# The wavelet stage in another order: TensorE's step in three runs, restoring and token work a step later, twelve input buffers

## The chip, the core and the metric

The kernel runs on one core of one Trainium2 chip. Five engines of the core run their own instruction queues, each strictly in the order in which the program wrote them: TensorE (PE; its weight loads are shown apart as PEld), VectorE (DVE), ScalarE (ACT), GpSimd (POOL) and the sync engine (SP), which here only issues DMAs. They meet at semaphores. The metric is the device time of one execution in microseconds, and the lower the better; the time of a kernel is the median of its runs.

## What is computed

The input `x` is a float32 tensor of 4 images, 64 channels, 128 by 128 points. Four blocks run one after the other, each with a residual sum:

```python
x = x + _L0_conv_ref(_ln_c(x), ...)      # Haar wavelet, 64x256 and 256x64 products, inverse wavelet
t = t + _L0_ffn_ref(_ln_t(t), ...)       # 32 experts, each picks the 8 best tokens of an image
x = x + _L1_conv_ref(_ln_c(x), ...)      # four directional scans with a 9-tap convolution
t = t + _L1_ffn_ref(_ln_t(t), ...)       # 8 experts, each token picks 2
```

The change touches only the program's first large stage. That stage takes `_ln_c` (mean and variance over the 64 channels of a point), the wavelet block as two matrix products ("low" and "restore") with the residual sum, which gives `x1`; and then, of `x1` as tokens, the layer norm `_ln_t`, the gate's logits and the running best eight of each expert. The later stages (expert choice, four scans, mixture) are as before.

## The kernel before

`wavelet_mixer` cuts the input into 64 chunks (`CHUNKS`) of 128 partitions by 512 columns (64 channels of an even and of an odd image row). Each engine has a loop over steps `c`; in a step it works on several chunks of different age. On TensorE a step of before holds, in this order:

- `centre(c)`, lines 412 and 413: `x` minus its mean over the channels, as two fp32r products, of the rounded part `xh` and of the rest `xl`, into the bank `xc`;
- `variance(c-1)`, lines 418 and 419: the same for the square of `xc`, parts `sqh` and `sql`, into `va`;
- `low(c-2)`, line 427: two f32 products that each use 64 columns of the array, into the bank `tv`;
- in even steps only, `gate_logits` (line 434, bank `lg`) and `token_variance` (line 441, bank `tv` again), for a pair of chunks, also 64 columns wide;
- `turn(c-3)`, line 455: four transposes of the finished `x1` into `tt`;
- `token_centre(c-4)`, lines 448 and 449: `x1` minus its mean, two fp32r products, parts `th` and `tl`, into `tc`;
- `restore(c-2)`, line 462: two f32 products of 256 columns into `rec`.

A step with the logits is called *heavy* below and one without them *light*; they alternate.

The other engines' parts of a step, in their order. ScalarE: `square(c)` (490), the logarithm of the variance (495), `copy_low(c-2)` (506, it empties the first half of `tv`), the exponential (499), `high_of_token(c-3)` (511, makes `th`), in even steps `token_rstd` (516 and 518), and `token_square(c-4)` (523). VectorE: `add_restored(c-3)` (581, makes `x1`), `high_of_square(c)` (588, makes `sqh`), `high_of_x(c+2)` (575), `scale_logits` (605) or `block_top` (611) in turn, `normalise(c-1)` (593), `copy_tokens(c-3)` (598). GpSimd has three subtractions: `low_of_square(c)` (545, makes `sql`), `low_of_x(c+2)` (550, makes `xl`), `low_of_token(c-3)` (556, makes `tl`). SP loads the chunk three steps ahead (367) and stores `x1` in two layouts (381 and 385).

So there is a ring through four engines: `centre` on TensorE, `square` on ScalarE, `high_of_square` on VectorE, then GpSimd, whose in-order queue has `low_of_square`, `low_of_x` and `low_of_token` behind one another, and back to TensorE. The wait with which `token_centre` takes the end of that queue is

```python
def token_centre(c):
    wait(pe, s["tparts"], c + 1)
    wait(pe, s["tsquared"], c)
```

and `token_variance(pair, c)`, which writes the bank that `low(c)` has just filled, waits for ScalarE's copy of it: `wait(pe, s["low_s"], min(c + 1, CHUNKS))`.

`metaformer_kernel` lays out the buffers and calls the stages; ten input buffers `xr` and ten semaphores `xin` go round.

Of the kernel before, what the change touches and what calls it, by code (L numbers as in the profile page):

```python
# [37 lines left out]
SLOT = B * HP * WP  # L38
TOK = HP * W
E0, HID, K0 = 32, 256, 8  # L40
XBUFS = 10
AHEAD = 3
E1 = 8
TAPS = 9
# [281 lines left out]

def wavelet_mixer(nc, g, a):

    LAG = 5
    PAIRS = CHUNKS // 2  # L330
    with ExitStack() as ctx:
        m = Mem(nc, ctx, "wm")
# [25 lines left out]
        with nc.Block() as block:  # L358
            @block.sync
            def _(sp):  # L360
                def load(c):
                    wait(sp, x1_out[c % XBUFS], c // XBUFS * 16)
                    wait(sp, s["tturned"], c - XBUFS + 1)
                    wait(sp, s["logits"], (c - XBUFS) // 2 * 2 + 2)
                    wait(sp, s["tparts"], c - XBUFS + 1)
                    for t in range(2):
                        sp.dma_start(buf(c)[t * C:t * C + C].rearrange("p (j w) -> p j w", j=JR),
                                     x_chunk(a, c, t)).then_inc(xin[c % XBUFS], 16)

                def load_experts(q):  # L370

                    e = slice(q * E0 // 8, (q + 1) * E0 // 8)
                    sp.dma_start(g.W1[0:C + 1, e], a["weight1"][e].rearrange("e d h -> d e h")
                                 ).then_inc(g.experts_loaded, 16)
                    for t in range(2):
                        sp.dma_start(g.W2[:, e, t, :], a["weight2"][e, t * P:t * P + P, :].rearrange(
                            "e p o -> p e o")).then_inc(g.experts_loaded, 16)

                def store_x1(c):
                    wait(sp, s["x1"], c + 1)  # L380
                    sp.dma_start(g.x1s[c:c + 1].rearrange("t p n -> p (t n)"), buf(c)).then_inc(x1_out[c % XBUFS], 16)

                def store_tokens(c):
                    wait(sp, s["tcopied"], c + 1)
                    sp.dma_start(tok_dst[c % B][:, c // B * JR:c // B * JR + JR, :],
                                 ts[c % 4].rearrange("p (j x) -> p j x", j=JR)).then_inc(tok_out[c % 4], 16)

                for sem in g.setup_sems:
                    sp.sem_clear(sem)
                for c in steps:  # L390
                    if now(c + AHEAD):
                        load(c + AHEAD)
                    if 8 <= c < 16:
                        load_experts(c - 8)
                    if now(c - 3):
                        store_x1(c - 3)
                    if now(c - 4):
                        store_tokens(c - 4)
                for u in range(XBUFS):
                    sp.wait_ge(x1_out[u], 16 * len(range(u, CHUNKS, XBUFS)))  # L400
                for u in range(4):
                    sp.wait_ge(tok_out[u], 16 * (CHUNKS // 4))
                sp.wait_ge(g.late_loaded, 16 * 6)

            @block.tensor
            def _(pe):
# [14 lines left out]
                def low(c):  # L421
                    wait(pe, s["normed"], c + 1)
                    wait(pe, s["low_s"], c)
                    wait(pe, s["tln"], (c - 3) // 2)
                    nv = nn[c % 2].rearrange("p (q v) -> p v q", v=2)
                    for v in range(2):
                        last = pe.matmul(tv[v * C:v * C + C, 0:N // 2], g.Alow[:, v], nv[:, v], start=True, stop=True)
                    last.then_inc(s["low"], 1)
# [8 lines left out]
                def token_variance(pair, c):  # L437
                    wait(pe, s["tsquared"], 2 * pair + 2)
                    wait(pe, s["low_s"], min(c + 1, CHUNKS))
                    for half in range(2):  # L440
                        last = pe.matmul(tv[half * C:half * C + C, :], g.J[:, C - E0:C + E0], tsq[half],
                                         start=True, stop=True)
                    last.then_inc(s["tvar"], 2)

# [21 lines left out]
                for c in steps:  # L466
                    if now(c):
                        centre(c)
                    if now(c - 1):
                        variance(c - 1)  # L470
                    if now(c - 2):
                        low(c - 2)
                    if now(c - 5) and c % 2 == 0:
                        gate_logits((c - 5) // 2)
                        token_variance((c - 5) // 2, c - 2)
                    if now(c - 3):
                        turn(c - 3)
                    if now(c - 4):
                        token_centre(c - 4)
                    if now(c - 2):  # L480
                        restore(c - 2)

            @block.scalar
            def _(act):
# [34 lines left out]

                def token_square(c):  # L520
                    wait(act, s["tcentred"], c + 1)
                    wait(act, s["tvar"], c - 1)
                    act.activation(tsq[c % 2], tc[:], ACT.Square).then_inc(s["tsquared"], 1)

                for c in steps:
                    if now(c):
                        square(c)
                    if now(c - 1):
                        log_of_variance(c - 1)
                    if now(c - 2):  # L530
                        copy_low(c - 2)
                    if now(c - 1):
                        rstd(c - 1)
                    if now(c - 3):
                        high_of_token(c - 3)
                    if now(c - 5) and c % 2 == 0:
                        token_rstd((c - 5) // 2)
                    if now(c - 4):
                        token_square(c - 4)

            @block.gpsimd
            def _(pool):
                def low_of_square(c):
                    wait(pool, s["high"], c + 1)
                    pool.tensor_tensor(sq_lo[:], sq[c % 2], sq_hi[:].bitcast(F32), ALU.subtract).then_inc(s["parts"], 1)  # L545

                def low_of_x(c):
                    wait(pool, s["xhigh"], c + 1)
                    wait(pool, s["centred"], c - 1)
                    pool.tensor_tensor(xl[c % 2][:], buf(c), xh[c % 2][:].bitcast(F32), ALU.subtract  # L550
                                       ).then_inc(s["xparts"], 1)

                def low_of_token(c):
                    wait(pool, s["thigh"], c + 1)
                    wait(pool, s["tcentred"], c - 1)
                    pool.tensor_tensor(tl[c % 2], buf(c), th[c % 2].bitcast(F32), ALU.subtract
                                       ).then_inc(s["tparts"], 1)
                for c in range(2):
                    low_of_x(c)
                for c in steps:  # L560
                    if now(c):
                        low_of_square(c)
                    if now(c + 2):
                        low_of_x(c + 2)
                    if now(c - 3):
                        low_of_token(c - 3)

            @block.vector
            def _(dve):
                dve.tensor_copy(Cmr[:], g.Cm[:]).then_inc(exact_ready, 1)  # L570

                def high_of_x(c):
                    wait(dve, xin[c % XBUFS], c // XBUFS * 32 + 32)
                    wait(dve, s["centred"], c - 1)
                    dve.tensor_copy(xh[c % 2][:], buf(c)).then_inc(s["xhigh"], 1)

# [36 lines left out]
                for c in range(2):  # L613
                    high_of_x(c)
                for c in range(CHUNKS + LAG + 2):
                    if now(c - 3):
                        add_restored(c - 3)
                    if now(c):
                        high_of_square(c)
                    if now(c + 2):  # L620
                        high_of_x(c + 2)
                    if now(c - 6) and c % 2 == 1:
                        scale_logits((c - 6) // 2)
                    if c >= 8 and c % 2 == 0:
                        block_top((c - 8) // 2)
                    if now(c - 1):
                        normalise(c - 1)
                    if now(c - 3):
                        copy_tokens(c - 3)

# [1151 lines left out]
def metaformer_kernel(nc, a, out):  # L1784
    g = Shared()
    with ExitStack() as ctx:
# [8 lines left out]
        g.experts_loaded, g.late_loaded = m.sem("experts_loaded"), m.sem("late_loaded")  # L1795

        g.mix_loaded = m.sem("mix_loaded")
        g.xin = m.sems("xin", XBUFS)
        g.taps_loaded, g.unit_ready, g.taps_turned, g.taps_hi, g.taps_cleared = (
            m.sem(f"w_{n}") for n in ("ld", "id", "tn", "hi", "clr"))  # L1800
        g.blank = {1: m.sem("w_b1"), 2: m.sem("w_b2")}
# [3 lines left out]

        v = Views(g.X, 0)
        g.xr = [v.take(N) for _ in range(XBUFS)]
        g.sq, g.rr, g.nn, g.tsq = ([v.take(N) for _ in range(2)] for _ in range(4))
        g.lowS = [v.take(N // 2) for _ in range(2)]
        g.ts = [v.take(N) for _ in range(4)]  # L1810
        g.trs = v.take(N)
# [60 lines left out]
```

## Time and profile before

| | us |
|---|---|
| time, median of 3 runs | 2098.15 (2095.51 to 2099.45) |
| the profiled execution | 2100.63 |
| its span in the trace | 2098.8 |
| TensorE busy | 1984.3 (95% of the span) |
| VectorE, ScalarE, GpSimd busy | 1201.0, 1035.5, 592.4 |
| wavelet stage, first chunk's second subtraction to the next stage's first instruction | about 18 to 316 |

The span runs from the first to the last instruction of the profile. An engine's busy time counts the length of its instructions; matmuls are pipelined, so that a TensorE that is busy all the time need not be at its peak, and where matmuls follow one another the distance of their starts says what one costs. In the wavelet stage TensorE is shown as busy without a gap, and the three other engines for 84 to 87% of the time.

### The profile page before, as it was taken

What the parts mean: (1) busy time and instruction counts of PE and PEld (TensorE: products, weight loads), DVE (VectorE), ACT (ScalarE), POOL (GpSimd) and SP (SyncE); (2) the same over time, 40 slices, a digit from 0 to 9 for tenths busy, and PEclk for the clock granted to TensorE, in tenths of its full rate; (3) what the DMA queues carried; (4) which work ended last, traced back from release to release, by engine and by line L of the source; (5) the groups of instructions that cost most, each with busy time, mean ns of one, the idle gap of its engine ahead of it and who ended that gap; (6) DMA issues with size and microseconds to landing.
All of it is one profiled execution on the core that took longest, in us unless ns stands there. A gap on an engine that the chain in (4) does not pass through costs nothing. (4 is left out here: it accounts for less than half of the span.)

```text
span 2098.8 us, 41975 instructions
## 1 busy us (share of the span) xinstructions
PE 1984.3 (95%) x14926; PEld 1531.5 (73%) x14926; DVE 1201.0 (57%) x2548; ACT 1035.5 (49%) x2879; POOL 592.4 (28%) x686
## 2 busy tenths in 40 slices
PE   6999991699999989999999999999999799999998
PEld 3555550377777779999999999999999544444443
DVE  5888879566666653222222222232222399999998
ACT  4888874343444413333344444444444555555552
POOL 5888864222222200000000000000000455555551
PEclk9999995699999999999999999999999799999999
DMA  4955540222232200000000000000000356666653
GB/s 113 259 178 179 176 148 16 86 92 98 84 101 91 92 22 1 0 0 0 0 3 0 0 0 0 20 0 0 0 0 0 90 150 158 161 159 156 161 147 89
DMA packets 192679, 159.14 MB, mean 76 GB/s; under 512 B 25848, under 2 KB 159000, under 8 KB 192536
## 3 DMA queue, kind: packets, MB, share of 16 engines
q1 hardware_dynamic: 190840, 156.89, 26.7%
q8 instruction: 66, 1.08, 0.2%
q0 software_dynamic: 512, 0.53, 0.1%
q14 instruction: 77, 0.63, 0.1%
q10 hardware_dynamic: 1184, 0.00, 0.0%
HBM read 56.70 MB, written 67.11 MB: 59 GB/s over the span
## 5 line engine op out<-in xcount | busy, mean ns | idle before, releaser
L1228 PE MATMUL s_ps<-g_ring,g_T 128*128 128x128 f32 x7620 | 856.9, 275 | 7.9 <-DVE g_ring L1275 7.9
L1228 PEld LDWEIGHTS s_ps<-g_ring,g_T 128*128 128x128 f32 x7620 | 855.7, 192 | 8.7 <-DVE g_ring L1275 8.5
L1264 DVE SCALAR_TENSOR_TENSOR g_ring<-s_ps,s_xs 128x128 f32<-128x128 f32 x508 | 148.5, 292 | 421.3 <-PE s_ps L1228 421.2
L1327 ACT ACTIVATE g_X<-g_ring 128x256 f32<-128x256 f32 x254 | 172.2, 678 | 298.8 <-DVE g_ring L1264 298.8
L1707 DVE TENSOR_TENSOR tm_Z<-tm_pg,tm_nd 128x1024 f32<-128x1024 f32 x256 | 301.4, 1209 | 7.3 <-PE tm_pg L1547 6.1
L1561 PE MATMUL tm_po<-tm_Z,g_wexp 128*64 128x512 f32 x1024 | 249.0, 607 | 0.0
L1311 ACT ACTIVATE g_X<-g_ring 64x256 f32 x256 | 106.9, 418 | 203.4 <-DVE g_ring L1264 201.1
L1264 DVE SCALAR_TENSOR_TENSOR g_ring<-s_ps,g_X 128x128 f32<-128x128 f32 x254 | 74.0, 291 | 209.5 <-PE s_ps L1228 209.5
L1643 POOL TENSOR_TENSOR g_X<-g_x,g_X 128x512 f32<-128x512 f32 x64 | 82.9, 1298 | 350.9 <-POOLq L1204 287.5
L1350 POOL MEMSET g_zero<- 128x1 f32 x1 | 0.1, 98 | 577.1 <-POOLq L1204 577.1
L1322 ACT ACTIVATE s_xs<-g_X 128x256 f32<-128x256 f32 x254 | 161.2, 636 | 0.6 <-PEq L1204 0.6
L1561 PEld LDWEIGHTS tm_po<-tm_Z,g_wexp 128*64 128x64 f32 x1024 | 62.5, 136 | 109.9 <-issue 108.0
L1024 PEld LDWEIGHTS af_ps<-g_yh,g_Tlo 128*128 128x128 f32 x635 | 85.0, 189 | 66.9 <-DVE g_yh L1135 54.4
L1620 ACT ACTIVATE tm_gT<-tm_bankB 64x512 fp32r<-64x512 f32 x64 | 37.8, 591 | 189.9 <-PE tm_bankB L1535 189.9
L1024 PE MATMUL af_ps<-g_yh,g_Tlo 128*128 128x256 f32 x635 | 111.5, 306 | 5.9 <-DVE g_yh L1135 4.2
L1135 DVE SCALAR_TENSOR_TENSOR g_yh<-af_ps,g_X 128x256 fp32r<-128x256 f32 x127 | 53.9, 425 | 90.4 <-PE af_ps L1028 87.9
L1547 PE MATMUL tm_pg<-tm_gT,g_sel 32*128 32x512 f32 x512 | 100.6, 464 | 1.3 <-DVE tm_Z L1707 1.2
L545 POOL TENSOR_TENSOR wm_sql<-g_X,wm_sqh 128x512 fp32r<-128x512 f32 x64 | 89.3, 1395 | 39.4 <-DVE wm_sqh L588 38.1
L1028 PE MATMUL af_ps<-g_yl,g_Thi 128*128 128x256 f32 x635 | 99.1, 287 | 0.0
L1024 PE MATMUL af_ps<-g_yh,g_Thi 128*128 128x256 f32 x635 | 97.8, 284 | 0.0
L1028 PEld LDWEIGHTS af_ps<-g_yl,g_Thi 128*128 128x128 f32 x635 | 86.6, 191 | 0.0
L1024 PEld LDWEIGHTS af_ps<-g_yh,g_Thi 128*128 128x128 f32 x635 | 85.9, 190 | 0.0
(277 smaller groups left out, 3001.9 us busy)
## 6 DMA issues: line engine op xcount, KB each, us to landing
tm_nd<-g_X SPq DMA_DIRECT2D x256, 128.0 KB, 2.4
g_X<-in_x SPq DMA_DIRECT2D x128, 128.0 KB, 2.8
x1s<-g_X SPq DMA_DIRECT2D x64, 256.0 KB, 2.1
x1tok<-g_X SPq DMA_DIRECT2D x64, 256.0 KB, 2.4
g_x<-x2s SPq DMA_DIRECT2D x64, 256.0 KB, 2.9
y<-tm_yo SPq DMA_DIRECT2D x128, 128.0 KB, 2.5
g_X<-x1s SPq DMA_DIRECT2D x32, 256.0 KB, 2.8
x2s<-g_X SPq DMA_DIRECT2D x32, 256.0 KB, 2.0
```

The source lines that it names most:

```text
L545: pool.tensor_tensor(sq_lo[:], sq[c % 2], sq_hi[:].bitcast(F32), ALU.subtract).then_inc(s["parts"], 1)
L1024: pe.matmul(out, t[:, d * P:d * P + P], g.yh[:, :, d:d + 64], start=(t is g.Tlo and d == 0), stop=False)
L1028: last = pe.matmul(out, g.Thi[:, d * P:d * P + P], g.yl[:, :, d:d + 64], start=False, stop=(d == ND - 1))
L1228: last = pe.matmul(out, g.T[i][:, d * P:d * P + P], g.ring[(u - 1) % RING][:, images(c), d:d + 64], start=(d == 0), stop=(d == ND - 1))
L1264: dve.scalar_tensor_tensor(g.ring[n % RING][:, images(c), inner], conv, 0.0, x[:, images(c)], ALU.max, ALU.add).then_inc(y_ready[c], 1)
L1311: last = act.activation(dst.rearrange("p b j w -> p b (j w)"), src, ACT.Copy)
L1322: act.activation(xs[n % RING][:], line(*place(n)), ACT.Copy).then_inc(staged, 1)
L1327: act.activation(line(*place(n)), g.ring[n % RING][:, :, inner], ACT.Copy).then_inc(stored, 1)
L1547: last = pe.matmul(pg[q % 2][:, h * N:h * N + N], sel[rows, at:at + 2].rearrange("p e c -> p (e c)"), gT[i][rows], start=True, stop=True)
L1561: last = pe.matmul(po[i][h * C:h * C + C, :], wexp[:, ep], Z[q % 4][:, h], start=False, stop=(ep == EP - 1), skip_group_check=True)
L1643: pool.tensor_tensor(xv, natural(x2[t % 2][i][:]), xv, ALU.add).then_inc(s["x3"], 1)
L1707: dve.tensor_tensor(Z[q % 4][:], pg[q % 2][:].rearrange("p (h n) -> p h n", h=2), nd[t % 2][i][:], ALU.mult).then_inc(s["z"], 1)
```

## The change

On TensorE a step is written in another order, and three of its items work on a chunk that is one step older. The six fp32r products (`centre`, `variance`, `token_centre`) come first, then all products of 64 columns (`low`, and in heavy steps `gate_logits` and `token_variance`), then transposes and `restore`. `restore` takes chunk `c-3` in place of `c-2`, `turn` `c-4`, `token_centre` `c-5`, and the heavy steps are the odd ones. All that follows `restore` moves a step with it on the other engines: `add_restored`, `copy_tokens`, the logits' scaling and the top eight on VectorE, `high_of_token` and `token_square` on ScalarE, `low_of_token` on GpSimd (it stays third in its step), the stores on SP. ScalarE's step is reordered too: the exponential directly behind the logarithm, then `token_square`, `high_of_token`, `copy_low`. `LAG` grows from 5 to 7; there are twelve input buffers on ten load semaphores and four buffers `tsq`.

TensorE, a heavy step of the middle of the stage, before, up to the next step's first product (`xc` is written by `centre`, `va` by `variance`, `tv` by `low` and `token_variance`, `lg` by the logits, `tt` by `turn`, `tc` by `token_centre`, `rec` by `restore`):

```order
L412 MATMUL wm_xc<-wm_xh,wm_Cmr 128x512
L413 MATMUL wm_xc<-wm_xl,wm_Cmr 128x512
L418 MATMUL wm_va<-wm_sqh,g_J 128x512
L419 MATMUL wm_va<-wm_sql,g_J 128x512
L427 MATMUL wm_tv<-g_X 64x256 x2
L434 MATMUL wm_lg<-g_X 64x512 x2
L441 MATMUL wm_tv<-g_X,g_J 64x512 x2
L455 MATMUL wm_tt<-g_X 128x128 x4
L448 MATMUL wm_tc<-wm_th,wm_Cmr 128x512
L449 MATMUL wm_tc<-wm_tl,wm_Cmr 128x512
L462 MATMUL wm_rec<-g_X 128x256 x2
```

And the same step of the changed kernel:

```order
L412 MATMUL wm_xc<-wm_xh,wm_Cmr 128x512
L413 MATMUL wm_xc<-wm_xl,wm_Cmr 128x512
L418 MATMUL wm_va<-wm_sqh,g_J 128x512
L419 MATMUL wm_va<-wm_sql,g_J 128x512
L448 MATMUL wm_tc<-wm_th,wm_Cmr 128x512
L449 MATMUL wm_tc<-wm_tl,wm_Cmr 128x512
L427 MATMUL wm_tv<-g_X 64x256 x2
L434 MATMUL wm_lg<-g_X 64x512 x2
L441 MATMUL wm_tv<-g_X,g_J 64x512 x2
L455 MATMUL wm_tt<-g_X 128x128 x4
L462 MATMUL wm_rec<-g_X 128x256 x2
```

The two products into `tc` moved from behind the transposes to directly behind the variance; everything else of the step now stands behind them.

ScalarE, a heavy step before (`wm_th` is `high_of_token`, the one that reads `wm_tc` is `token_square`, the one of 128x256 is `copy_low`, 516 and 518 are `token_rstd`):

```order
L490 ACTIVATE g_X<-wm_xc 128x512
L495 ACTIVATE g_X<-wm_va,g_eps 128x512
L506 ACTIVATE g_X<-wm_tv,g_b 128x256
L499 ACTIVATE g_X<-g_X 128x512
L511 ACTIVATE wm_th<-g_X 128x512
L516 ACTIVATE g_X<-wm_tv,g_eps 128x512
L518 ACTIVATE g_X<-g_X 128x512
L523 ACTIVATE g_X<-wm_tc 128x512
```

And the same step of the changed kernel:

```order
L490 ACTIVATE g_X<-wm_xc 128x512
L495 ACTIVATE g_X<-wm_va,g_eps 128x512
L499 ACTIVATE g_X<-g_X 128x512
L523 ACTIVATE g_X<-wm_tc 128x512
L511 ACTIVATE wm_th<-g_X 128x512
L506 ACTIVATE g_X<-wm_tv,g_b 128x256
L516 ACTIVATE g_X<-wm_tv,g_eps 128x512
L518 ACTIVATE g_X<-g_X 128x512
```

`copy_low` moved from third place to behind `token_square` and `high_of_token`. GpSimd's queue reads alike in both, three subtractions to a step; only the chunk of the third is a step older.

The core of the diff:

```diff
-XBUFS = 10
+XBUFS, XSEMS = 12, 10
-    LAG = 5
+    LAG = 7
...
-                    if now(c - 3):
-                        store_x1(c - 3)
                     if now(c - 4):
-                        store_tokens(c - 4)
+                        store_x1(c - 4)
+                    if now(c - 5):
+                        store_tokens(c - 5)
...
                     if now(c - 1):
                         variance(c - 1)
+                    if now(c - 5):
+                        token_centre(c - 5)
                     if now(c - 2):
                         low(c - 2)
-                    if now(c - 5) and c % 2 == 0:
-                        gate_logits((c - 5) // 2)
-                        token_variance((c - 5) // 2, c - 2)
+                    if now(c - 6) and c % 2 == 1:
+                        gate_logits((c - 7) // 2)
+                        token_variance((c - 7) // 2, c - 2)
+                    if now(c - 4):
+                        turn(c - 4)
                     if now(c - 3):
-                        turn(c - 3)
-                    if now(c - 4):
-                        token_centre(c - 4)
-                    if now(c - 2):
-                        restore(c - 2)
+                        restore(c - 3)
...
                     if now(c - 1):
                         log_of_variance(c - 1)
+                    if now(c - 1):
+                        rstd(c - 1)
+                    if now(c - 5):
+                        token_square(c - 5)
+                    if now(c - 4):
+                        high_of_token(c - 4)
                     if now(c - 2):
                         copy_low(c - 2)
-                    if now(c - 1):
-                        rstd(c - 1)
-                    if now(c - 3):
-                        high_of_token(c - 3)
-                    if now(c - 5) and c % 2 == 0:
-                        token_rstd((c - 5) // 2)
-                    if now(c - 4):
-                        token_square(c - 4)
+                    if now(c - 6) and c % 2 == 1:
+                        token_rstd((c - 7) // 2)
...
                     if now(c + 2):
                         low_of_x(c + 2)
-                    if now(c - 3):
-                        low_of_token(c - 3)
+                    if now(c - 4):
+                        low_of_token(c - 4)
...
-                    if now(c - 3):
-                        add_restored(c - 3)
+                    if now(c - 4):
+                        add_restored(c - 4)
...
-        g.sq, g.rr, g.nn, g.tsq = ([v.take(N) for _ in range(2)] for _ in range(4))
+        g.sq, g.rr, g.nn = ([v.take(N) for _ in range(2)] for _ in range(3))
+        g.tsq = [v.take(N) for _ in range(4)]
```

## Rows read from the trace of the kernel before

**Rows 1.** Stretches: their ends, then length; each engine's busy us; PEclk; DMA.

```profile
100.00:300.00 200.00, 200.00 (x996) 118.02 (x996) 169.13 (x315) 168.31 (x316) 173.64 (x134) 1.00 0.56 174
300.00:316.00 16.00, 11.78 (x58) 5.28 (x54) 9.28 (x16) 9.34 (x17) 3.85 (x3) 1.00 0.36 115
```

**Rows 2.** Timeline of TensorE, light then heavy step: start, us, engine, line, instruction.

```profile
152.54 1.03 PE L462 MATMUL wm_rec<-g_X 128*128 128x256 f32 x4
...
153.64 0.40 PE L413 MATMUL wm_xc<-wm_xl,wm_Cmr 128*128 128x512 f32 x1
...
156.00 1.03 PE L462 MATMUL wm_rec<-g_X 128*128 128x256 f32 x4
...
157.32 0.39 PE L413 MATMUL wm_xc<-wm_xl,wm_Cmr 128*128 128x512 f32 x1
...
157.78 0.40 PE L419 MATMUL wm_va<-wm_sql,g_J 128*128 128x512 f32 x1
158.11 0.67 PE L427 MATMUL wm_tv<-g_X 128*64 128x256 f32 x4
158.61 1.02 PE L434 MATMUL wm_lg<-g_X 128*64 128x512 f32 x4
159.47 1.06 PE L441 MATMUL wm_tv<-g_X,g_J 128*64 128x512 f32 x4
160.46 0.66 PE L455 MATMUL wm_tt<-g_X 128*128 128x128 f32 x4
160.87 0.48 PE L448 MATMUL wm_tc<-wm_th,wm_Cmr 128*128 128x512 f32 x1
...
162.51 0.40 PE L413 MATMUL wm_xc<-wm_xl,wm_Cmr 128*128 128x512 f32 x1
```

**Rows 3.** Timeline of ScalarE, VectorE and GpSimd beside the same steps.

```profile
154.08 0.60 ACT L490 ACTIVATE g_X<-wm_xc 128x512 f32<-128x512 f32 x1 [0.55 <-PE wm_xc L413]
...
154.70 0.43 DVE L588 CAST wm_sqh<-g_X 128x512 fp32r<-128x512 f32 x1 [0.22 <-ACT g_X L490]
...
155.21 1.41 POOL L545 TENSOR_TENSOR wm_sql<-g_X,wm_sqh 128x512 fp32r<-128x512 f32 x1 [0.75 <-DVE wm_sqh L588]
...
156.18 0.69 DVE L593 TENSOR_TENSOR g_X<-wm_xc,g_X 128x512 f32<-128x512 f32 x1
...
156.57 1.29 POOL L550 TENSOR_TENSOR wm_xl<-g_X,wm_xh 128x512 fp32r<-128x512 f32 x1
...
157.82 1.28 POOL L556 TENSOR_TENSOR wm_tl<-g_X,wm_th 128x512 fp32r<-128x512 f32 x1
...
158.38 1.01 DVE L588 CAST wm_sqh<-g_X 128x512 fp32r<-128x512 f32 x1
```

**Rows 4.** Timeline of ScalarE in the same steps: two in a row, and `copy_low`.

```profile
156.04 0.62 ACT L511 ACTIVATE wm_th<-g_X 128x512 fp32r<-128x512 f32 x1
156.57 0.58 ACT L523 ACTIVATE g_X<-wm_tc 128x512 f32<-128x512 f32 x1
...
158.83 0.47 ACT L506 ACTIVATE g_X<-wm_tv,g_b 128x256 f32<-128x256 f32 x1
```

**Rows 5.** Timeline of TensorE and its loads where `token_centre` waited, at the stage's end.

```profile
310.52 0.19 PEld L448 LDWEIGHTS wm_tc<-wm_th,wm_Cmr 128*128 128x128 f32 x1 [1.38 <-POOL wm_tl L556]
...
310.86 0.40 PE L449 MATMUL wm_tc<-wm_tl,wm_Cmr 128*128 128x512 f32 x1
```

**Rows 6.** Timeline: `centre` of chunks 7 and 63, the stage's last instruction on VectorE.

```profile
46.73 0.59 PE L412 MATMUL wm_xc<-wm_xh,wm_Cmr 128*128 128x512 f32 x1
...
295.18 0.58 PE L412 MATMUL wm_xc<-wm_xh,wm_Cmr 128*128 128x512 f32 x1
...
315.28 0.69 DVE L611 MAX8 g_cand<-g_E 128x8 f32<-128x512 f32 x1
```

## What is expected of the change

> **What bounds the kernel now.** I first read the stretches of the wavelet stage [rows 1]: over 200 us of its middle TensorE shows 200.00 us busy, the others 168 to 174. So TensorE's step sets the pace, if its time is work. The distance of starts in its timeline tells that [rows 2]. From the second `centre` product of the light step (153.64) to that of the next light step (162.51) are 8.87 us: one pair of steps. A fp32r product costs 0.23 (two from 157.32 to 157.78). From `variance` to `low` are 0.33; `low` to the logits 0.50; logits to `token_variance` 0.86; from there to the transposes 0.99. `restore` up to the second `centre` product is 1.10 (152.54 to 153.64), but 1.32 the other time (156.00 to 157.32): there `centre` waits for `normalise` on VectorE, which ends at 156.18 + 0.69 = 156.87 [rows 2, 3]. So 0.22 of the 8.87 is a wait, 8.65 is TensorE's own.
>
> Then I read the ring that feeds it [rows 3]. After the light step's second `centre` product (153.64) `square` starts at 154.08, the cast to `sqh` at 154.70, GpSimd's three subtractions at 155.21, 156.57 and 157.82, and the third, `tl`, ends at 159.10. That is 5.46 us after the product. `tl` goes to `token_centre` of the following heavy step, which reads it at 160.87: 1.77 us of slack, because in that step it stands behind `low`, logits, `token_variance` and transposes. That order is what keeps this wait out of the profile.
>
> **The change part by part.** *Three runs.* No product is added or removed. The array changes between 128 and 64 columns twice per step before, and twice after. Those places are where starts lie further apart (0.33 in place of 0.23 ahead of `low`), and both stay. The distance around `token_centre` (160.46 to 162.51 = 2.05, of which 0.47 are its own two products and 1.10 `restore` up to the second `centre`) leaves 0.48 for the transposes, and nothing for the change of kind: grouping by kind is worth 0.
>
> *`restore` a step later.* `copy_low` gets a step more, and `centre` no longer meets `normalise` so late: at best the 0.22 per pair, 32 pairs, 7.0 us. This is the whole gain on offer.
>
> *`token_centre` early.* It now stands directly behind `variance`. In the timeline of before that place of the heavy step is 158.01 (157.78 + 0.23), and `tl` ends at 159.10 [rows 2, 3]: 1.1 us too late. Giving `token_centre` a chunk one step older doesn't help: `low_of_token` went a step later with it, and is still the third subtraction of GpSimd's step, behind a `low_of_square` that needs this step's `centre`. Queued behind the waiting product on TensorE are `low`, logits, `token_variance`, transposes, `restore` and the next `centre`; for that `centre` wait ScalarE, VectorE and again GpSimd. So the wait closes a loop, once per pair, from the light step's second `centre` product to that of the next light step:
> - to the end of `tl`: 5.46 [rows 2, 3];
> - the start of `token_centre` behind it, 0.06, an estimate between 0.03 and 0.1, and from a waiting start to its second product 0.34 (310.52 to 310.86) [rows 5];
> - second product to `low` 0.33, `low` 0.50, logits 0.86, `token_variance` 0.99, transposes 0.48, `restore` and first `centre` 1.10 [rows 2]: 4.26.
>
> Together 10.12 us in place of 8.87.
>
> *ScalarE's order.* `copy_low` now stands behind `token_square` and `high_of_token`, and `token_variance` waits for it, since both use the bank `tv`. From `token_centre`'s second product: 0.40 to its end, 0.03 for the hand-over (154.68 to 154.70 between `square` and the cast) [rows 3], then `token_square` and `high_of_token` at the distance 0.53 of two such instructions (156.04 to 156.57), `copy_low` 0.47, and up to 0.17 to `token_variance` (159.30 to 159.47, where it may not have been what was waited for) [rows 2, 4]. That is 2.13 at most, 1.96 at least. TensorE itself needs 0.33 + 0.50 + 0.86 = 1.69. So 0.27 to 0.44 more; I take 0.36. The loop is then 10.48 us. That the exponential now stands directly behind the logarithm and waits for its end costs ScalarE some 0.1 per step, off this loop.
>
> *Buffers and DMA.* The loads stay three steps ahead. They wait for the chunk that had the buffer before: `x1` is stored and read a step later, and two more buffers give two steps. DMA share is 0.56 [rows 1] and SP's stores move with `x1`. Cost 0; were the buffers too few, a load would show on VectorE's `high_of_x`. The two more `tsq` only lift a wait.
>
> *Head and end.* From `centre(7)` to `centre(63)` are 28 pairs: 295.18 - 46.73 = 248.45 us = 28 x 8.87 [rows 6]. After: 28 x 10.48 = 293.4, **+45**. Ahead of that the first logits come a step later while the first waits begin: -2 to +1, I take -1. From `centre(63)` to the last `block_top` are 20.8 us now (315.28 + 0.69 - 295.18) [rows 6]. The end becomes longer: step 63 turns from light to heavy and a fourth heavy step follows. At least that is the work that comes to stand behind `centre(63)`, one chunk's `token_centre`, transposes and `restore` (0.47 + 0.48 + 0.87) and one pair's logits and variance (0.86 + 0.99): 3.7. At most it is a whole heavy step with its wait, 7, and 1 us of hand-overs. I take 7, near the upper end, as the same queue still makes the waits there.
>
> Sum: 45 - 1 + 7 = **+51 us**. Of the profiled execution (2100.63) that makes 2151.6; the median of the runs lies 2.5 lower, at 2098.15, and the forecast with it: **2149 us**, 2.4% slower. Without ScalarE's part the pair is 10.12, 28 x 1.25 = 35, with -2 and +3.7 about +37: 2135. The upper end is 10.6 per pair (hand-overs of 0.1 more in each lap), 28 x 1.73 + 1 + 8 = +57: 2155.
>
> In the ring the cast to `sqh` stands once with 0.43 and once with 1.01 us [rows 3]: the long one begins at 158.38, while GpSimd still runs `tl`, and ends 0.29 after it; the short one finds GpSimd idle. On the loop it is the light step's cast, the short one, since GpSimd has long finished there. The Trainium skill (SBUF — State Buffer, "SBUF: two separate sides") says that VectorE's faster copy modes and GpSimd share a pair of ports as an exclusive lock: the loser waits for the other's whole instruction. The two rows agree. By that rule a cast that met a subtraction in the new order would lose to it, and that is the second rival.
>
> **The rivals.** *Not slower.* If `tl` came in time, the change would earn its 0.22 per pair and pay only the longer end: 2098.15 - 28 x 0.22 + 3.7 = about 2096. It decides where the ring's 5.46 us are no longer than what TensorE needs from the light step's second `centre` product to behind the heavy step's `variance`: 158.01 - 153.64 - 0.22 = 4.15. So 1.3 us would have to go, a whole subtraction of GpSimd. Against it stands the queue's fixed order and that its three starts follow one another by 1.36 and 1.25 with no idle time. 4%.
>
> *The cast on the loop meets a subtraction.* The light step's cast takes 1.01 in place of 0.43: 0.58 x 28 = 16 more, 2165. It decides if `tl` of the heavy step's own turn ends later than the light step's `square`, which needs GpSimd to fall behind; but a longer pair gives GpSimd more idle time. 5%.
>
> *The clock falls.* TensorE now stands still for over 1 us in each pair. If its granted clock dropped from 2.4 to 1.2 GHz, the 4.6 us of its own work on the loop would double: 28 x 4.6 = 129 more, about 2280. Against it: in the stage's last 16 us TensorE is busy for 11.78 only and is granted 1.00 throughout [rows 1]. 3%.
>
> *A part of the loop gives way* (GpSimd's ends are rough in a profile, and ScalarE's part may be hidden): a pair of 9.4 to 10.0, 2113 to 2132. 6%.
>
> **How the numbers follow.** The forecast, a loop of 10.1 to 10.6 us, has 82%, and 2135 to 2155. The range of 8 in 10 takes a few us of slack at either end for the head and the end of the stage: 2133 to 2159. A measurement of this kernel can tell about 0.2%, 4 us, from no change. Faster by more has 2% (half of the first rival, were the end shorter than I count), no change 2%, slower 96%.
>
> **What the changed profile would show.** Right: TensorE's pair of steps at about 10.5 us, light steps near 3.4 and heavy ones near 7; a new wait of `token_centre` (lines 448) for GpSimd's `tl` in every heavy step, over 1 us, and a small one of `token_variance` for `copy_low`; GpSimd idle ahead of `low_of_square` for over 2 us once per pair; granted clock 1.00. Wrong: no wait at `token_centre` and pairs under 9 us; or waits at VectorE's `high_of_x` for loads, which would say that the buffers and not the queue decide; or a long cast in the light step.

## The result

The changed kernel takes 2148.74 us (median of 4 runs, 2147.43 to 2150.29) against 2098.8 us of the kernel before (4 runs, the three of before and one more): a ratio of 1.0237, interval 1.0224 to 1.025. It is slower by 50 us. The forecast was 2149 us, between 2133 and 2159.

This is the stretch of the wavelet stage's middle, with the columns of [rows 1] (busy us of TensorE, its loads, VectorE, ScalarE, GpSimd; granted clock; DMA share):

```profile
100.00:300.00 200.00, 174.35 (x843) 98.38 (x844) 145.55 (x268) 148.57 (x268) 147.69 (x115) 1.00 0.50 152
```

In the same 200 us all engines do less: TensorE has 843 matmul records where it had 996, and is busy for 174 us where [rows 1] had 200.00. So no engine is full with work; they wait for one another in turn. The granted clock is 1.00 as before.

The timeline of TensorE tells where they wait, from a light step's second `centre` product to that of the next light step (columns as in [rows 2]; in brackets the idle time ahead and who ended it):

```profile
156.77 0.39 PE L413 MATMUL wm_xc<-wm_xl,wm_Cmr 128*128 128x512 f32 x1
...
159.11 1.03 PE L462 MATMUL wm_rec<-g_X 128*128 128x256 f32 x4
...
160.25 0.40 PE L413 MATMUL wm_xc<-wm_xl,wm_Cmr 128*128 128x512 f32 x1
...
160.72 0.39 PE L419 MATMUL wm_va<-wm_sql,g_J 128*128 128x512 f32 x1
162.27 0.50 PE L448 MATMUL wm_tc<-wm_th,wm_Cmr 128*128 128x512 f32 x1 [1.16 <-POOL wm_tl L556]
162.61 0.39 PE L449 MATMUL wm_tc<-wm_tl,wm_Cmr 128*128 128x512 f32 x1
162.93 0.68 PE L427 MATMUL wm_tv<-g_X 128*64 128x256 f32 x4
163.44 1.03 PE L434 MATMUL wm_lg<-g_X 128*64 128x512 f32 x4
164.67 1.08 PE L441 MATMUL wm_tv<-g_X,g_J 128*64 128x512 f32 x4 [0.20 <-ACT g_X L506]
165.68 0.66 PE L455 MATMUL wm_tt<-g_X 128*128 128x128 f32 x4
166.17 1.03 PE L462 MATMUL wm_rec<-g_X 128*128 128x256 f32 x4
...
167.26 0.39 PE L413 MATMUL wm_xc<-wm_xl,wm_Cmr 128*128 128x512 f32 x1
```

The pair takes 167.26 - 156.77 = 10.49 us (8.87 in [rows 2]): 3.48 for the light step, 7.01 for the heavy one. Two waits stand in it, both new: `token_centre` for GpSimd's `tl`, and `token_variance` for ScalarE's `copy_low` (164.06 to 164.53 on ScalarE). The idle time in brackets reads short here: the matmul ahead of the wait still counts as busy. Starts tell the whole cost: `token_centre` could have begun 0.23 after 160.72, at 160.95, and began 1.32 later, where the bracket says 1.16.

GpSimd's timeline beside it shows the other end of the first wait, ScalarE's (`copy_low`) that of the second:

```profile
158.34 1.40 POOL L545 TENSOR_TENSOR wm_sql<-g_X,wm_sqh 128x512 fp32r<-128x512 f32 x1 [2.39 <-DVE wm_sqh L588]
159.71 1.28 POOL L550 TENSOR_TENSOR wm_xl<-g_X,wm_xh 128x512 fp32r<-128x512 f32 x1
160.96 1.26 POOL L556 TENSOR_TENSOR wm_tl<-g_X,wm_th 128x512 fp32r<-128x512 f32 x1
```

```profile
164.06 0.47 ACT L506 ACTIVATE g_X<-wm_tv,g_b 128x256 f32<-128x256 f32 x1
```

`tl` ends at 160.96 + 1.26 = 162.22, which is 5.45 us after the light step's second `centre` product at 156.77; `token_centre` starts 0.05 behind it. And GpSimd, the engine that is waited for, has just stood idle for 2.39 us: its queue holds the second and third subtraction behind the first, and the first needs `sqh`, which comes from this step's `centre`.

The list of waits over the same 200 us (engine, what waited, for whom; us in total, times, longest) shows that they return in every pair:

```profile
POOL wm_sql L545 <- DVE wm_sqh L588: 52.7, 39, 2.4
...
PE wm_tc L448 <- POOL wm_tl L556: 21.9, 19, 1.2
...
PE wm_tv L441 <- ACT g_X L506: 3.8, 19, 0.2
```

All 19 heavy steps of the stretch wait. For the stage as a whole, these are the lines of [rows 6] in the changed kernel (`centre` of chunks 7 and 63 and the last `block_top`):

```profile
45.13 0.58 PE L412 MATMUL wm_xc<-wm_xh,wm_Cmr 128*128 128x512 f32 x1
...
338.20 0.47 PE L412 MATMUL wm_xc<-wm_xh,wm_Cmr 128*128 128x512 f32 x1
...
365.99 0.69 DVE L611 MAX8 g_cand<-g_E 128x8 f32<-128x512 f32 x1
```

Up to `centre` of chunk 7 the changed kernel is 1.6 us ahead (45.13 for 46.73), the 28 pairs take 293.07 in place of 248.45, 44.6 more, and the end from `centre(63)` takes 28.5 in place of 20.8, 7.7 more. Together the stage ends 50.7 us later. The spans differ by 49.7 (2148.5 and 2098.8), so the stages behind give back 1.0, which lies within the spread of the runs.

### The profile page after: what moved, and what is told of

It reads as the page before. It is cut to its first block and busy times, and to the rows that moved or that the text cites. A ratio compares the mean times of both kernels' runs of the same rounds, so it can differ in the third digit from the quotient of the medians.

```text
span 2148.5 us, 41970 instructions
## 1 busy us (share of the span) xinstructions
PE 1992.5 (93%) x14926; PEld 1528.9 (71%) x14926; DVE 1203.7 (56%) x2548; ACT 1045.3 (49%) x2879; POOL 591.1 (28%) x686
## 5 line engine op out<-in xcount | busy, mean ns | idle before, releaser
L598 DVE COPY g_X<-wm_tt 128x512 f32<-128x512 f32 x64 | 44.0, 688 | 75.4 <-PE wm_tt L455 75.4
```

## The experiments

The theory has two terms: the early place of `token_centre` closes a loop through GpSimd's third subtraction, and `copy_low`'s late place on ScalarE lengthens that loop. The rivals are that the greater ages of the chunks, and with them the longer pipeline, cost the time; that the buffers do; that the order of the products itself gives or takes something; and that ScalarE's branch runs beside the loop and costs nothing. Pairs are measured from a light step's second `centre` product (line 413) to that of the next light step.

**One part of the change alone, in the kernel before.** `token_centre` directly behind `variance`, all else as before:

```diff
                     if now(c - 1):
                         variance(c - 1)
+                    if now(c - 4):
+                        token_centre(c - 4)
                     if now(c - 2):
                         low(c - 2)
...
-                    if now(c - 4):
-                        token_centre(c - 4)
                     if now(c - 2):
                         restore(c - 2)
```

> The kernel before, with one part of the change alone: token_centre (c-4, its age as before) directly behind variance. Ages, ScalarE's order, buffers as before. Theory (the early place closes the ring through GpSimd's third subtraction): 5.46 + 0.06 + 0.34 + 4.26 = 10.1 us per pair of steps, since copy_low is not behind token_square here; 28 pairs x 1.25 = 35 more and some us at the end: 2134 to 2140 us, a wait of token_centre for GpSimd of about 0.5 to 1.2 us per pair. Rival (the step more of age of restoring and token work, with the longer head and end, makes the loss): no wait, about 2099 us.

Measured: 2138.49 us, ratio 1.019 (1.0173 to 1.0207). Its timeline of TensorE, from a light step's second `centre` product to that of the next light step, and the `tl` that it waits for:

```profile
150.59 0.39 PE L413 MATMUL wm_xc<-wm_xl,wm_Cmr 128*128 128x512 f32 x1
...
154.42 0.47 PE L412 MATMUL wm_xc<-wm_xh,wm_Cmr 128*128 128x512 f32 x1 [0.21 <-DVE g_X L593]
...
156.09 0.50 PE L448 MATMUL wm_tc<-wm_th,wm_Cmr 128*128 128x512 f32 x1 [0.51 <-POOL wm_tl L556]
...
158.12 1.06 PE L441 MATMUL wm_tv<-g_X,g_J 128*64 128x512 f32 x4
...
160.69 0.39 PE L413 MATMUL wm_xc<-wm_xl,wm_Cmr 128*128 128x512 f32 x1
```

```profile
154.75 1.29 POOL L556 TENSOR_TENSOR wm_tl<-g_X,wm_th 128x512 fp32r<-128x512 f32 x1
```

The pair is 10.10 us, the loop without ScalarE's part: `tl` ends at 156.04, 5.45 us after the product at 150.59, and the way back takes the other 4.65. `token_variance` doesn't wait. `token_centre` waits for `tl` for less than in the changed kernel (0.51 for 1.16 in the brackets), because the heavy step's `centre` has already waited for VectorE's `normalise` (line 593); that wait lies inside the same lap. Neither ages nor buffers are changed here, and 40 of the 50 us are there: the place alone makes them.

**The reader a step later.** The changed kernel, but `token_centre` and `token_square` take a chunk one step older:

```diff
-                    if now(c - 5):
-                        token_centre(c - 5)
+                    if now(c - 6):
+                        token_centre(c - 6)
...
-                    if now(c - 5):
-                        token_square(c - 5)
+                    if now(c - 6):
+                        token_square(c - 6)
```

> The changed kernel with token_centre and token_square taking the chunk one step older (c-6 in place of c-5), everything else as changed. tl is then ready a whole step ahead. Theory: the wait of token_centre for GpSimd is gone. The second term stays and grows: in a heavy step copy_low still stands behind the exponential, token_square and high_of_token, and nothing else holds token_variance now, so it waits for copy_low for over 1 us per heavy step; pair about 9.9, 2127 to 2134 us. If ScalarE's order were no term of its own: pair 8.65, about 2096. Rival (the ages make the loss): slower than the changed kernel, over 2150.

Measured: 2130.05 us, ratio 1.0143 (1.0126 to 1.016). TensorE in its heavy step, and ScalarE beside it:

```profile
153.42 0.40 PE L413 MATMUL wm_xc<-wm_xl,wm_Cmr 128*128 128x512 f32 x1
...
154.12 0.39 PE L448 MATMUL wm_tc<-wm_th,wm_Cmr 128*128 128x512 f32 x1
...
155.17 1.03 PE L434 MATMUL wm_lg<-g_X 128*64 128x512 f32 x4
157.20 1.08 PE L441 MATMUL wm_tv<-g_X,g_J 128*64 128x512 f32 x4 [1.00 <-ACT g_X L506]
```

```profile
155.06 0.63 ACT L499 ACTIVATE g_X<-g_X 128x512 f32<-128x512 f32 x1
155.59 0.58 ACT L523 ACTIVATE g_X<-wm_tc 128x512 f32<-128x512 f32 x1
156.07 0.62 ACT L511 ACTIVATE wm_th<-g_X 128x512 fp32r<-128x512 f32 x1
156.59 0.47 ACT L506 ACTIVATE g_X<-wm_tv,g_b 128x256 f32<-128x256 f32 x1
```

The wait for GpSimd is gone, and the kernel is faster than the changed one though an age is a step greater still: the rival of the ages falls. But only 19 us come back, since the wait for `copy_low` has grown from 0.37 to 1.17 us (155.17 to 157.20 less the 0.86 of the logits). `copy_low` ends at 157.06 and `token_variance` starts 0.14 behind it. With the first wait out of the way, the second sets the pair, at 9.86 us. From the heavy step's second `centre` product to `token_variance` are 3.78 us (153.42 to 157.20), the way through ScalarE's queue.

**`copy_low` one place earlier.** The changed kernel with `copy_low` between `token_square` and `high_of_token`:

```diff
                     if now(c - 5):
                         token_square(c - 5)
+                    if now(c - 2):
+                        copy_low(c - 2)
                     if now(c - 4):
                         high_of_token(c - 4)
-                    if now(c - 2):
-                        copy_low(c - 2)
```

> The changed kernel with copy_low one place earlier on ScalarE, between token_square and high_of_token; the rest as changed. Theory: the small wait of token_variance for copy_low goes (0.53 less on that branch against 0.37 of waiting), the wait of token_centre for GpSimd stays; pair 10.49 to about 10.1, 28 x 0.37 = 10 less and a little at the end: 2134 to 2140 us. Rival (ScalarE's branch runs beside the loop and costs nothing): unchanged, 2149.

Measured: 2138.17 us, ratio 1.0189 (1.0172 to 1.0206). TensorE, the pair's first and last product and `token_variance`:

```profile
152.15 0.39 PE L413 MATMUL wm_xc<-wm_xl,wm_Cmr 128*128 128x512 f32 x1
...
159.67 1.06 PE L441 MATMUL wm_tv<-g_X,g_J 128*64 128x512 f32 x4
...
162.24 0.40 PE L413 MATMUL wm_xc<-wm_xl,wm_Cmr 128*128 128x512 f32 x1
```

The pair is 10.09 us, and `token_variance` no longer waits. ScalarE's branch costs what was counted, 0.4 us a pair and 10.6 us in all, and lies on the loop, not beside it.

**GpSimd's queue in another order.** The changed kernel with `low_of_token` ahead of `low_of_x`:

```diff
-                    if now(c + 2):
-                        low_of_x(c + 2)
                     if now(c - 4):
                         low_of_token(c - 4)
+                    if now(c + 2):
+                        low_of_x(c + 2)
```

> The changed kernel with GpSimd's subtractions in the order low_of_square, low_of_token, low_of_x. Theory: the ring to token_centre is up to 1.25 us shorter, so the pair falls from 10.49 to between 9.2 (if only this counts) and 9.9 (if th on ScalarE, which now is needed earlier, and token_variance's wait for copy_low take over): 2112 to 2133 us. Rival (loss from ages or from the products' order itself, not from GpSimd's queue): unchanged, 2149.

Measured: 2128.93 us, ratio 1.0145 (1.0128 to 1.0162), pair 9.85 us. No instruction is saved, and 20 us come back. The list of waits over 100 to 300 us still names both:

```profile
PE wm_tv L441 <- ACT g_X L506: 7.3, 20, 0.4
PE wm_tc L448 <- POOL wm_tl L556: 7.2, 20, 0.4
```

Only the upper one sets the pair. These are the heavy step's second `centre` product and `token_variance`:

```profile
151.58 0.40 PE L413 MATMUL wm_xc<-wm_xl,wm_Cmr 128*128 128x512 f32 x1
...
155.36 1.08 PE L441 MATMUL wm_tv<-g_X,g_J 128*64 128x512 f32 x4 [0.37 <-ACT g_X L506]
```

They lie 3.78 us apart, just as with the reader a step later, where `token_centre` waits for nothing and the pair is 9.86; and in neither trace is `token_square` listed as waiting for `token_centre`'s products. So what is left of the wait for `tl` is hidden behind ScalarE's queue, and both experiments stop at the same second loop.

**A part of the suspected cost.** The changed kernel with `low_of_token` on 256 of the 512 columns; the rest of `tl` is set to zero once, before the stage's first product (two `memset` and their wait are not shown):

```diff
-                    pool.tensor_tensor(tl[c % 2], buf(c), th[c % 2].bitcast(F32), ALU.subtract
+                    pool.tensor_tensor(tl[c % 2][:, 0:N // 2], buf(c)[:, 0:N // 2], th[c % 2][:, 0:N // 2].bitcast(F32), ALU.subtract
```

> The changed kernel with GpSimd's low_of_token on the left 256 of 512 columns only (the right half of tl stays zero, so the token mean is less exact there; TensorE's products are whole). A dose of the suspected cost: that subtraction falls from 1.28 to about 0.66. Theory: the loop shortens by the same 0.6 us, pair 10.49 to 9.9, 28 x 0.6 = 17 and 1 to 3 us at the end less: 2128 to 2133 us. Rival (GpSimd's queue is not on the loop): unchanged, 2149.

Measured: 2133.08 us, ratio 1.0164 (1.0149 to 1.018). One pair on TensorE, and the groups of GpSimd over 100 to 300 us (instructions of a line with shapes and count; busy us, mean ns; idle before):

```profile
151.55 0.40 PE L413 MATMUL wm_xc<-wm_xl,wm_Cmr 128*128 128x512 f32 x1
...
161.49 0.40 PE L413 MATMUL wm_xc<-wm_xl,wm_Cmr 128*128 128x512 f32 x1
```

```profile
L545 POOL TENSOR_TENSOR wm_sql<-g_X,wm_sqh 128x512 fp32r<-128x512 f32 x40 | 56.0, 1401 | 65.9 <-DVE wm_sqh L590 65.9
...
L556 POOL TENSOR_TENSOR wm_tl<-g_X,wm_th 128x256 fp32r<-128x256 f32 x41 | 29.7, 725 | 0.0
```

The subtraction takes 0.725 us, not the 0.66 I had counted, about 0.55 less than the 1.28 of the whole one; the pair is 9.94 us, 0.55 less than 10.49. What is taken off GpSimd's third subtraction comes off the pair one for one, though GpSimd is idle for 1.65 us ahead of each `low_of_square` on average (65.9 / 40).

**The buffers.** The kernel before with twelve input buffers on ten load semaphores (`XBUFS, XSEMS = 12, 10`).

> The kernel before with twelve input buffers on ten load semaphores, nothing else. Theory: no load is waited for before or after, so nothing changes: 2099 us within 4. Rival (buffers or their addresses matter): more than 4 us away.

Measured: 2098.08 us, ratio 1.0003 (0.9993 to 1.0013). Within 0.1% the buffers cost nothing and bring nothing by themselves.

**Both terms out.** The changed kernel with the reader a step later, as above, and in heavy steps ScalarE in another order:

```diff
...
-                    if now(c - 1):
+                    heavy = c % 2 == 1
+                    if now(c - 1) and not heavy:
                         rstd(c - 1)
-                    if now(c - 5):
-                        token_square(c - 5)
+                    if now(c - 6):
+                        token_square(c - 6)
+                    if now(c - 2) and heavy:
+                        copy_low(c - 2)
+                    if now(c - 1) and heavy:
+                        rstd(c - 1)
                     if now(c - 4):
                         high_of_token(c - 4)
-                    if now(c - 2):
+                    if now(c - 2) and not heavy:
                         copy_low(c - 2)
```

> The changed kernel with both terms taken out: token_centre and token_square one step older (c-6), and in heavy steps ScalarE in the order token_square, copy_low, exponential, high_of_token (light steps as changed). Theory: TensorE waits for nothing, the pair is its own 8.65 us; against the kernel before 0.22 less per pair, 28 x 0.22 = 6 less, and 2 to 4 more at the longer end: 2094 to 2098 us, 0.1 to 0.2% faster than before. The three runs by kind bring nothing of their own: if they did, the pair would come under 8.65. Rival (ages and the longer pipeline cost): at or over 2105.

Measured: 2094.39 us (11 runs), ratio 0.9979 (0.9968 to 0.9989): faster than the kernel before, by 0.2%. TensorE, light and heavy step:

```profile
154.59 0.40 PE L413 MATMUL wm_xc<-wm_xl,wm_Cmr 128*128 128x512 f32 x1
...
158.07 0.39 PE L413 MATMUL wm_xc<-wm_xl,wm_Cmr 128*128 128x512 f32 x1
...
158.76 0.40 PE L448 MATMUL wm_tc<-wm_th,wm_Cmr 128*128 128x512 f32 x1
159.00 0.39 PE L449 MATMUL wm_tc<-wm_tl,wm_Cmr 128*128 128x512 f32 x1
159.32 0.67 PE L427 MATMUL wm_tv<-g_X 128*64 128x256 f32 x4
159.82 1.03 PE L434 MATMUL wm_lg<-g_X 128*64 128x512 f32 x4
160.68 1.07 PE L441 MATMUL wm_tv<-g_X,g_J 128*64 128x512 f32 x4
...
163.27 0.39 PE L413 MATMUL wm_xc<-wm_xl,wm_Cmr 128*128 128x512 f32 x1
```

No matmul waits, and the pair is 8.68 us. This is the same order of products on TensorE as in the changed kernel, the same three runs by kind. So the order itself costs nothing; and as 8.68 is not under the 8.65 that the kernel before needs without its wait for `normalise`, it saves nothing of its own either. What this kernel earns is that wait, 0.2 us a pair. Whether the later `restore` or the earlier exponential takes it out, no run tells apart. Over the 28 pairs it is 5.3 us; up to `centre(7)` another 2.0 are gained, and the end, where the longer pipeline has to be paid, takes back 4.1 (24.9 us from `centre(63)` in place of 20.8). That leaves 3.1 of the 3.6 us measured.

## Why the prediction held

- **The gain on offer, 0.22 us per pair.** Right, and not reached by the change: behind the light step, where `restore` to the second `centre` product took 1.32 [rows 2], it now takes 1.14 (159.11 to 160.25), so most of that wait is gone; it shows as a gain only where both new waits are out. The trace of before lists no wait there, and the prediction had it from starts alone; the run with the early place alone lists it 20 times in 200 us (`centre` for line 593, 0.21 in its lines).
- **Grouping by kind, 0.** Right, by the 8.68 us above.
- **The loop's first lap, 5.46 us to the end of `tl`.** Measured 5.45. It was read off the kernel before, where TensorE did not wait for that lap's end; none of its instructions changed its duration by more than 0.03, or its place ahead of the next one.
- **The way back, 4.26 + 0.06 + 0.34.** Measured from 162.22 to 167.26: 5.04, less the 0.37 of ScalarE's part, 4.67 for 4.66.
- **ScalarE's part, 0.36 (0.27 to 0.44).** Measured 0.37 (163.44 to 164.67 is 1.23, less 0.86). The hand-over of 0.03 reads as 0.02 in the row that it names, and took 0.04 here; the sum does not hang on it. The experiment that removed it gained 10.6 us, where 28 times that are 10.4.
- **The pair, 10.48 and 28 times that, +45.** Measured 10.49 and +44.6.
- **Head -1, end +7.** Measured -1.6 and +7.7. The end was the weakest term, chosen near the upper bound and not derived step by step; that it came near is in part luck. In the trace `token_centre` still waits for GpSimd three times behind `centre(63)`, which fits the choice. Two experiments show its parts: with the early place alone the end takes 24.2 us, 3.4 more than before; with both terms out, and so the longer pipeline without the waits for `tl`, it takes 24.9, 4.1 more. Together that is 7.5 of the 7.7, though the second has its reader a step older still.
- **The time, 2149.** Measured 2148.74. That the two lie 0.3 us apart is luck too: single runs of this kernel spread over 2.9 us, and the stages behind gave back 1.0 that was not forecast.
- **The cast with a short and a long form.** In the changed kernel the light step's cast takes 0.43 and the heavy one's, which begins while `tl` runs, 1.19:

```profile
157.83 0.43 DVE L588 CAST wm_sqh<-g_X 128x512 fp32r<-128x512 f32 x1 [0.21 <-ACT g_X L490]
...
161.32 1.19 DVE L588 CAST wm_sqh<-g_X 128x512 fp32r<-128x512 f32 x1
```

The long one ends at 162.51, 0.29 after `tl` (162.22), by the same distance as in [rows 3]. Both casts agree with the lock that the Trainium skill states (SBUF — State Buffer, "SBUF: two separate sides"); no run isolates it. The cast that is long is not on the loop, and the rival that the light step's cast would be caught did not come about.
- **The other rivals.** The clock stayed at 1.00 in the 200 us of the middle in spite of a stop in each pair. "Not slower" fell on its own condition: `tl` came 1.3 us too late. No part of the loop gave way: the pair is 10.49 us, and each part has its counted length within 0.04.

One thing in the expectation of the half subtraction was off: half the columns do not take half the time (0.725 of 1.28 us); the theory's own statement, that the pair shortens by as much as the subtraction, held.

## What to carry to other kernels

A full engine is a floor, not a schedule: before moving an instruction ahead, look at when its input is ready in the trace of before, and count the slack that its old place gave (here 1.77 us) against the distance that it moves (here 160.87 to 158.01, 2.86 us: 1.1 too far). Where the input is the last of several in an in-order queue on another engine, giving the reader older data helps only if the producer does not grow older with it; and a single wait that stands in front of the instruction that starts the next round is paid in every round. Look for a second wait behind the first: taking out one of two here brought back 19 or 11 of 50 us, and both together 54.

## What was not expected

GpSimd's subtraction of 256 columns took 0.725 us and of 512 columns 1.28 us in the same stage: by a straight line through these two sizes, 0.17 us of it does not depend on the columns.
